# Two segment softmaxes of a graph kernel: both exponents from one difference, split by two Relus on ScalarE

## What is computed

```python
# layer 3 (L2_gnn)
score = jnp.einsum('ehd,ehd->eh', q[dst], k[src]) / math.sqrt(HD)
score = score + edge_attr @ We + be
m = jax.ops.segment_max(score, dst, num_segments=n)
exp_s = jnp.exp(score - m[dst])
ssum = jax.ops.segment_sum(exp_s, dst, num_segments=n)
attn = exp_s / (ssum[dst] + 1e-08)
msg = attn[..., None] * v[src]
out = jax.ops.segment_sum(msg, dst, num_segments=n)
out = out.reshape(n, D) @ Wo + bo
h = out + residual          # then two layer norms
# layer 4 (L3_gnn)
alpha = jnp.where(alpha >= 0, alpha, 0.2 * alpha)
amax = jax.ops.segment_max(alpha, dst, num_segments=n)
ex = jnp.exp(alpha - amax[dst])
denom = jax.ops.segment_sum(ex, dst, num_segments=n)
msg = v[src] * (ex / (denom[dst] + 1e-16))[:, :, None]
out = jax.ops.segment_sum(msg, dst, num_segments=n)
```

## Time and profile before

| | us |
|---|---|
| median of 3 runs | 3909.14 (3906.57 to 3911.62) |
| the profiled execution | 3892.84, its span 3891.1 |
| hop 4, first to last scan of the maximum | 2609.46 to 3252.38 |
| hop 5, the same | 3312.79 to 3852.24 |
| the last scatter of hop 5 starts | 3881.55 |

### The profile page before, as it was taken

The page is one execution under the profiler, slowest core; times in us unless marked ns, Lnnn a source line. Parts: engine busy times, 40 slices in busy tenths (PEclk is TensorE's granted clock), DMA queues, the critical chain, the costliest instruction groups (busy, mean ns, idle before and its releaser), DMA issues. The chain is left out here.

```text
span 3891.1 us, 48029 instructions
## 1 busy us (share of the span) xinstructions
PE 2681.5 (69%) x11826; PEld 1733.3 (45%) x11826; DVE 3381.2 (87%) x7569; ACT 2534.8 (65%) x5535; POOL 2446.9 (63%) x2202
## 2 busy tenths in 40 slices
PE   5877877778861688865656545547888885776774
PEld 4555555555540344435545534424444442444442
DVE  5999999999987788858868869969999996998886
ACT  3788788878862466645646646637777775565554
POOL 4565566666650566517767767757766651788777
PEclk9999999999985677767676775659999887666555
DMA  3888877766652988837868868832333221433332
GB/s 102 195 197 199 199 197 199 199 197 194 203 177 79 252 253 258 253 110 239 270 196 257 261 203 252 248 122 81 90 86 87 83 77 52 112 96 92 95 95 65
DMA packets 402066, 644.05 MB, mean 166 GB/s; under 512 B 127455, under 2 KB 207720, under 8 KB 401790
## 3 DMA queue, kind: packets, MB, share of 16 engines
q1 hardware_dynamic: 332030, 527.96, 45.1%
q0 software_dynamic: 69760, 113.02, 11.9%
HBM read 347.78 MB, written 296.81 MB: 166 GB/s over the span
## 5 line engine op out<-in xcount | busy, mean ns | idle before, releaser
L1607 POOL DMA_INDIRECT gs_g<-table_xw,slot_idx x588 | 612.2, 1041 | 297.7 <-issue 257.0
L898 POOL DMA_INDIRECT gs_t<-table_x,slot_idx x392 | 439.7, 1122 | 310.9 <-POOLq L83 125.4
L507 POOL DMA_INDIRECT gs<-x,src_idx x200 | 219.5, 1098 | 342.1 <-DMA xd_rows<-gd 249.3
L1274 POOL DMA_INDIRECT slot_idx<-node_map,src_idx x200 | 242.9, 1214 | 192.7 <-DMA slot_idx<-node_map,src_idx 91.7
L378 PE MATMUL ps<-ident,own_g 128*128 128x128 f32 x588 | 139.8, 382 | 251.5 <-DVE own_g L1709 251.2
L1653 ACT ACTIVATE hT_g<-u_g 128x512 f32<-128x512 f32 x147 | 92.5, 629 | 330.9 <-DVE u_g L1721 330.7
L507 POOL DMA_INDIRECT gd<-x,dst_idx x200 | 243.9, 1220 | 60.9 <-issue 59.1
L1883 POOL DMA_INDIRECT out<-x_t,end_idx x196 | 234.6, 1197 | 59.9 <-issue 59.0
L495 POOL DMA_INDIRECT node_map<-slot_no,end_idx x200 | 222.9, 1114 | 61.0 <-issue 60.6
L898 POOL DMA_INDIRECT own_t<-table_x,own_idx x196 | 222.2, 1134 | 59.7 <-issue 59.4
L1714 DVE TENSOR_TENSOR_SCAN agg_g<-same_seg,agg_g,ps 128x512 f32<-128x512 uint8 x147 | 187.3, 1274 | 48.5 <-PE ps L378 48.2
(11 more groups left out here) (366 smaller groups left out, 9514.9 us busy)
## 6 DMA issues: line engine op xcount, KB each, us to landing
table_xw<-xw_b SPq DMA_DIRECT2D x147, 512.0 KB, 4.8
...
own_g<-table_xw SPq DMA_DIRECT2D x147, 256.0 KB, 4.3
...
```

Source lines behind the costliest of these rows:

```text
L507: pool.indirect_dma_start(out=to[k % 3][:, j * D:(j + 1) * D], out_offset=None, in_=x, in_offset=bass.IndirectOffsetOnAxis(ap=of[:, n:n + ...
L898: pool.indirect_dma_start(out=self.B[L % RING][g][:, t * D:(t + 1) * D], out_offset=None, in_=table, in_offset=bass.IndirectOffsetOnAxis(a ...
L1274: pool.indirect_dma_start(out=slot_idx[:, t:t + 1], out_offset=None, in_=node_map, in_offset=bass.IndirectOffsetOnAxis(ap=src_idx[:, t:t + ...
L1607: pool.indirect_dma_start(out=gs[c % 6][:, j * D:(j + 1) * D], out_offset=None, in_=tables[layer], in_offset=bass.IndirectOffsetOnAxis(ap= ...
```

## The change

M[j] is the larger of m0 = min(pen, M[j-1]) and the score. With d = score - m0 it follows that M - m0 = relu(d) and M - score = relu(-d). So F = exp(-relu(d)) and p = exp(-relu(-d)), and one difference does for both. VectorE writes m0 to F and d to p and no longer subtracts M twice. ScalarE, which took two exponentials, takes a Relu into F, a Relu of -d in place into p (it waits for the first, which reads p), and then the two exponentials with scale -1, F first. In the table of hop 4 the place of `sums` goes from 192 to 195, `turn_sums` keeps 218, and hop 5 has the same places as before. The score in PSUM is now let go by the later of VectorE's two instructions (`dz`).

```diff
         V.tensor_tensor_scan(b["M"][:, 1:CH + 1], b["pen"][:], limit, b["M"][:, 0:1], ALU.min, ALU.max).then_inc(S("M"), 1)
         step.due(v, "M", L)
-        V.tensor_tensor(b["p"][:], score, b["M"][:, 1:CH + 1], ALU.subtract).then_inc(S("dz"), 1)
         V.tensor_tensor(b["F"][:], b["pen"][:], b["M"][:, 0:CH], ALU.min).then_inc(S("Dm0"), 1)
         step.due(v, "Dm0", L)
-        V.tensor_tensor(b["F"][:], b["F"][:], b["M"][:, 1:CH + 1], ALU.subtract).then_inc(S("Dm"), 1)
+        V.tensor_tensor(b["p"][:], score, b["F"][:], ALU.subtract).then_inc(S("dz"), 1)
 
     def run_weights(act, step, b, L):
 
         step.due(act, "dz", L)
-        nc.scalar.activation(b["p"][:], b["p"][:], ACT.Exp).then_inc(S("p"), 1)
-        step.due(act, "Dm", L)
-        nc.scalar.activation(b["F"][:], b["F"][:], ACT.Exp).then_inc(S("F"), 1)
+        nc.scalar.activation(b["F"][:], b["p"][:], ACT.Relu).then_inc(S("rise"), 1)
+        step.due(act, "rise", L)
+        nc.scalar.activation(b["p"][:], b["p"][:], ACT.Relu, scale=-1.0).then_inc(S("drop"), 1)
+        nc.scalar.activation(b["F"][:], b["F"][:], ACT.Exp, scale=-1.0).then_inc(S("F"), 1)
+        step.due(act, "drop", L)
+        nc.scalar.activation(b["p"][:], b["p"][:], ACT.Exp, scale=-1.0).then_inc(S("p"), 1)
...
-                "maximum": (157, "M_first M dz Dm0 Dm"), "gather": (-420, ""), "exps": (172, "p F"),
-                "sums": (192, "msg den num"), "scores_e": (54, ""), "turn_sums": (218, "den_rows"), "divisor": (276, "dn rd"),
+                "maximum": (157, "M_first M Dm0 dz"), "gather": (-420, ""), "exps": (172, "rise drop F p"),
+                "sums": (195, "msg den num"), "scores_e": (54, ""), "turn_sums": (218, "den_rows"), "divisor": (276, "dn rd"),
...
-                "maximum": (204, "M_first M dz Dm0 Dm"), "exps": (228, "p F"), "sums": (272, "msg den num"),
+                "maximum": (204, "M_first M Dm0 dz"), "exps": (228, "rise drop F p"), "sums": (272, "msg den num"),
```

## The result

The changed kernel takes 4028.47 us (median of 4 runs, 4025.39 to 4035.84), the kernel before beside it on the same chip 3907.86 us. The ratio is 1.0313 (95% interval 1.0293 to 1.0332), some 122 us (120.6 by the medians). The forecast was 27.5 us more, with 3963 us as the upper end. The direction was right; the size lies far outside the range.

A forecast was written before the change was run, and what follows sets the result against it. VectorE was taken to bound hop 4 (96% busy), POOL hop 5. Terms 3.3 (hop 4 start) + 13.4 (hop 4 periods) + 4.8 (hop 5 start) + 6 (POOL) = 27.5 us on 3909.14 gave 3936.6 us, range 3910 to 3963.

The forecast's parts named there:

- The clean period: Hop 4 chunk with VectorE back to back, 13.20 us before: claimed 13.30 us, 0.10 us more.
- Message at S+6.53: Clean period of hop 4: message starts 6.53 us after S, the start of the scan of the maximum; before, S+5.84.
- the wait for Wo: Hop 4, VectorE ahead of `h_res`: a new wait of 0.66 us for TensorE's product with Wo.
- The disturbed periods: The third of hop 4's periods lengthened by waits: 0.65 us more each; with the clean ones 13.4 us over 48 periods.
- the disturbances grow: Rival, hop 4: Wo at the lower clock takes 2.08 us, on VectorE's path; 28 us there, 3967 us in all; chance 0.22.
- Starts: First chunks of hops 4 and 5, where nothing covers the longer chain: 3.3 us and 4.8 us more.
- POOL's pace: Hop 5: POOL's indirect DMAs meet other VectorE scans; 6 us more, sign uncertain.
- A shift of the mean by 0.05 us: Sign of being wrong: POOL's mean operation time moving by over 0.05 us, 20 us by itself.
- I take the 6: Hop 5, choice for POOL: the later 200 operations cost 0.03 us more each, 6 us, as VectorE stops in a regular place.
- The bound of 22 us: Hop 5, second half: one more scan met by POOL in each chunk, 24 x 0.93, costs 22 us.
- The even case: Rival: all hop 4 periods clean (4.8 us), POOL 11 us better; 2 us more in all, 3911 us; chance 0.17.

The follow-up runs named there:

- hop 4 alone: Changed functions used in hop 4 only (sums at 195), hop 5 as in the kernel before: ratio 1.0266, 104 us more.
- the filler: Changed hop 4 with two unused 128-row products (448 and 256 columns) ahead of Wk and Wq, hop 5 as in the kernel before: ratio 0.9995.
- hop 5 alone: Changed functions used in hop 5 only, hop 4 as in the kernel before: ratio 1.0062, 24 us; run again, 1.0055.
- the old order with such work: Kernel before with an unused product of 128 rows by 448 columns ahead of the scores and another ahead of Wo in hop 4: ratio 0.9976.
- three Relus: Kernel before, all subtractions kept, with three Relus over p ahead of hop 5's table load and exponents: ratio 0.9997, run again 1.0033.

## Why the prediction was wrong, and where it was right

**The clean period** of hop 4 was right: 13.30 us forecast, 13.3 in the four periods at full clock of hop 4 alone and in all with the filler. Message at S+6.53 forecast, S+6.57 in the latter; the wait for Wo 0.66 forecast, 0.58 found.

**The disturbed periods** are the step that failed. I wrote "with a third of the periods disturbed", at 0.65 us more each, and bounded the case that all are at 31 us; where 13.4 us were forecast it cost 101. Two things are wrong in it. The share was taken from the kernel before as if it were a constant, but it goes with the clock: with the clock held no disturbed period is left in the old order, and with the change all 90 matmuls with Wk are at the lower clock, not 31. That it is the idle time moved ahead of Wk (1.75 us in the clean periods, nothing before the change) that lowers the clock there is argued and not shown: filling it with 128 rows brings the clock up, and taking it away brings Wk up; but four periods of hop 4 alone had it at the full clock. And for a disturbed period I shifted VectorE's chain by what ScalarE did later, without closing the loop. The loop through TensorE's four products at the lower clock and ScalarE's whole row of work, with the Relus in it, is 16.4 us; it could be summed from the rows at hand (the products at the lower clock were in the trace, shows one). The rival "the disturbances grow" had the right cause, the lower clock, at a quarter of its price, since it too held the share at a third and priced one product, with Wo, which was not the one that counted. What it had against itself, that the low stretches "mostly lie later in the period", the trace of the kernel before doesn't bear out: of 90 matmuls each, 31 with Wk and 30 with Wq are at the lower clock, 24 of the scores and 27 of the query.

That the clock is the cause and not a by-product rests on two results: in one kernel the same code runs at 13.3 and then at 15 to 16.4 us with the clock's step, and 1.5 us of added products of 128 rows take nearly all of the loss of hop 4 away.

**Starts.** Hop 4's first message comes 6.60 us after its first scan (2620.20 to 2626.80); forecast 6.53, before 3.25. Hop 5's first scatter waits 4.94 us for it instead of 0.47, so 4.5 us against 4.8 forecast; 10.96 us a chunk in the first half against 10.98. The nearness of 4.5 and 4.8 is in part luck, since that wait is 0.3 to 2.1 us in most profiles with the old hop 5.

**POOL's pace** was mis-sized: 6 us forecast, 392 x 0.055 = 21.6 found between the two profiles, and by the ratios of hop 5 alone 22 to 24 us for the start and the pace together, where 10.8 were forecast. A shift of the mean by 0.05 us was the sign of being wrong that I had named. "I take the 6" rested on the slower stretch's mean of 1.229 us for the late half. The late half went to 1.297, a rhythm that neither stretch of the earlier trace rows had. The bound of 22 us, one more scan met a chunk in the second half, was near the 21.6, and the reason to prefer the low end (a fixed cycle in the slower stretch) was the wrong way round: a fixed cycle makes each meeting cost in every chunk. What fixes the cycle stays open. By what the Trainium skill, SBUF — State Buffer, section Who interferes with whom, infers for tensor_tensor, an instruction with two SBUF inputs doesn't hold up descriptor generation, and this term would be nothing; the gather at 1.76 us beside the scan of the denominator speaks against it once more.

**The even case** (all periods clean) is what hop 4 comes to with the clock up, 0.9995 with the filler, though not for the reason that I gave, POOL's better pace: it takes added work, and the old order with such work is faster still, 0.9976.

Open remain why the clock falls when it does, what fixes the rhythm of hop 5, and what three Relus cost there.

## What to carry to other kernels

Where a TensorE product stands in a loop with other engines, sum the loop twice, with products at the higher and at the lower clock, and ask whether the change moves TensorE's idle time ahead of products in that loop: the share of slow periods in the trace before is no constant of the kernel. If TensorE idles ahead of a product, a filler of 128 rows that fits into that idle time may pay (0.9 us of work a chunk bought 6 to 10 us here), one of 33 rows didn't, and one placed where TensorE doesn't idle cost 6 to 8 us. Beside a queue of indirect DMAs, count for each chunk which VectorE scans they meet and at what offset, and expect that a fixed rhythm can repeat the worst meeting. And take a stage's length from more than one profile: the old hop 5 varied by 15 us over seven.

## What the runs showed of the chip

- The same program text in the same hop ran four periods at the full clock and then, without a visible cause, over forty at a mean of 0.76; the products with Wk went from 1.10 to 2.05 us. Within each of those periods the clock comes back: the product with Wo takes 1.16 us there.
- A TensorE that is 94% busy with the 33-row products added was granted 0.74; one 84% busy with 128-row products added 0.99, one 88% busy 1.00.
- An indirect DMA on POOL takes 0.99 us alone and 1.5 to 1.8 us (1.93 in the earlier trace rows) in some of its meetings with a VectorE scan. Of 118 such overlaps in hop 4 of the kernel before 92 cost next to nothing (under 1.1 us), and the 22 that took over 1.5 us started some 0.1 us after the scan had.
